# The expert stage: weights given back and loaded in pieces, in a new order of TensorE's work

## The reference

```
scores = sigmoid(x @ router.T)               # 32 experts, 4 chosen per token out of 3 of 8 groups
for each expert e: its first 10 tokens are taken (C = ceil(1.25 * 256 / 32) = 10), Xp[e] is 10 x 512
G = Xp @ W_gate[e]; U = Xp @ W_up[e]         # 512 x 256 each
Y = (silu(G) * U) @ W_down[e]                # 256 x 512
out[token] += weight * Y                     # scatter back
out += (silu(x @ sg.T) * (x @ su.T)) @ sd.T  # shared expert, hidden width 512
```

## Time and profile before

| | |
|---|---|
| median of 3 runs | 696.8 us (695.75 to 697.35) |
| profiled execution: its time, its span | 695.87 us, 694.0 us |
| mean granted clock of TensorE | 0.975 |
| busy: TensorE, VectorE, ScalarE, GpSimd | 631.8, 386.7, 360.5, 187.5 us |
| transfers over the whole span | 105.13 MB, 151 GB/s in the mean |
| expert stage, from the first row product to the end | 595.2 to 694.0 us |

### The profile page before, as it was taken

The page is one execution under the profiler, slowest core; times in us unless marked ns, Lnnn a source line. Parts: engine busy times, 40 slices in busy tenths (PEclk is TensorE's granted clock), DMA queues, the critical chain, the costliest instruction groups (busy, mean ns, idle before and its releaser), DMA issues.

```text
span 694.0 us, 14831 instructions
## 1 busy us (share of the span) xinstructions
PE 631.8 (91%) x5841; PEld 457.0 (66%) x5892; DVE 386.7 (56%) x536; ACT 360.5 (52%) x517; POOL 187.5 (27%) x151
## 2 busy tenths in 40 slices
PE   6999899999999999999999999999978988899855
PEld 5977666777777777777777777985546875553211
DVE  4869587767767677767677766341136854300001
ACT  3532766667666676667666766861126862110000
POOL 0250333443344334433442444440002220000000
PEclk9999999999999999999999999999989997999989
DMA  9934964324315305206215224009970051199993
GB/s 353 418 112 86 282 206 92 64 42 98 73 25 112 72 9 128 59 12 133 47 28 120 46 45 105 2 8 405 418 302 35 0 211 64 44 418 418 418 417 132
DMA packets 25511, 105.13 MB, mean 151 GB/s; under 512 B 3968, under 2 KB 7296, under 8 KB 19584
## 3 DMA queue, kind: packets, MB, share of 16 engines
q1 hardware_dynamic: 25472, 104.57, 46.1%
HBM read 77.29 MB, written 0.52 MB: 112 GB/s over the span
## 4 chain that ended last, share of the span: by engine, by line
PE 63%; DVE 14%; issue 10%; DMA 4%; SPq 4%; ACT 4%; POOL 1%; DVEq 0%; ACTq 0%
DVE arena L744 8%; PE psO L1044 6%; PE psM L994 6%; PE psO L1035 5%; PE psO L1036 5%; PE psS L1022 5%; PE psS L1023 5%; PE psO L1114 4%; SPq L366 4%; PE psO L979 3%; DMA arena<-w_exp 3%; PE psO L949 2%; PE psS L1255 2%; PE psS L957 2%; PE psO L980 2%
## 5 line engine op out<-in xcount | busy, mean ns | idle before, releaser
L707 DVE TENSOR_REDUCE arena<-psM 128x2 f32<-128x1024 f32 x121 | 148.3, 1225 | 80.9 <-PE psM L994 80.6
L425 POOL TENSOR_TENSOR arena<-arena 128x1024 bf16<-128x1024 f32 x64 | 138.4, 2163 | 147.5 <-ACT arena L531 143.5
L530 ACT ACTIVATE arena<-psS 128x1024 bf16<-128x1024 f32 x128 | 132.3, 1033 | 26.0 <-PE psS L1023 13.7
L1035 PE MATMUL psO<-arena 128*128 128x129 bf16 x1024 | 132.8, 220 | 1.5 <-ACT arena L530 1.2
L531 ACT ACTIVATE arena<-psS 128x1024 f32<-128x1024 f32 x128 | 132.6, 1036 | 0.0
L1036 PE MATMUL psO<-arena 128*128 128x128 bf16 x1024 | 132.3, 220 | 0.0
L1022 PE MATMUL psS<-arena 128*128 128x256 bf16 x512 | 120.5, 273 | 0.9 <-DVE arena L718 0.9
L1023 PE MATMUL psS<-arena 65*128 65x256 bf16 x512 | 120.8, 273 | 0.0
L1035 PEld LDWEIGHTS psO<-arena 128*128 128x128 bf16 x1024 | 99.1, 98 | 20.9 <-issue 12.7
L1036 PEld LDWEIGHTS psO<-arena 128*128 128x128 bf16 x1024 | 99.4, 97 | 6.7
L744 DVE TENSOR_TENSOR arena<-arena 128x1024 bf16<-128x1024 f32 x64 | 82.2, 1285 | 20.8 <-ACT arena L531 20.8
(11 more groups left out here) (188 smaller groups left out, 743.5 us busy)
## 6 DMA issues: line engine op xcount, KB each, us to landing
arena<-w_exp SPq DMA_DIRECT2D x32, 1024.0 KB, 17.1
arena<-arena SPq DMA_DIRECT2D x96, 256.0 KB, 3.8
arena<-w_exp SPq DMA_DIRECT2D x32, 512.0 KB, 17.9
arena<-w_pair SPq DMA_DIRECT2D x8, 1088.0 KB, 16.4
arena<-w_o SPq DMA_DIRECT2D x1, 4096.0 KB, 18.4
arena<-ctx SPq DMA_DIRECT2D x4, 512.0 KB, 12.9
arena<-rope SPq DMA_DIRECT2D x4, 512.0 KB, 13.6
arena<-w_shared_in SPq DMA_DIRECT2D x1, 2048.0 KB, 8.4
```

Of the source, the lines that this page charges most:

```text
L425: nc.gpsimd.tensor_tensor(p_lo[:, s % 2, :], p_f[:, s % 2, :], p_hi[:, s % 2, :], ALU.subtract).then_inc(s_plo[0], 1)
L530: nc.scalar.activation(p_hi[:, s % 2, :], psS[s % 2][:, :], ACT.Exp).then_inc(s_phi, 1)
L707: nc.vector.reduce_max(maxes[:, :, st, c], maxima_bank(q, m)[:, :].rearrange("p (j n) -> p j n", j=2), AX.X).then_inc(s_mfree, 1)
L1035: mm(psC[:, st, :], ph, vx[:, GROUP * g + i, 0:CW], start=g == 0 and i == 0 and st == 0, stop=False, skip_group_check=True)
```

## The change

1. **Row products and gate-up are interleaved.** TensorE starts a row product when the first half of the one-hot is there, and does gate-up of group 0 quarter by quarter, one row product behind. Group 1's gate-up follows at once; shared products 1 and 2 come behind down(0) and down(1), shared product 3 and weights_by_slot into group 2, shared_out(0 to 3) into groups 3 to 6.
2. **The first two groups give back quarters.** SyncE loads experts 13 to 20 (the places of groups 0 and 1) as 32 transfers of 256 KB, each quarter as soon as its gate-up quarter is done (`gu_part`); then the eight down parts, then expert 12, which now comes after both groups. Experts 21 to 28 are loaded as before.
3. **The last three experts** (29 to 31) come as 4 x 3 quarters of gate-up and 2 x 3 column halves of down (256 KB each, two runs of 1 KB in a row), each with a semaphore of its own, and gate-up of group 7 waits by quarters.
4. **The last trio is done in column halves**: down of groups 6 and 7 writes columns 0 to 255 into `psA[0]` and 256 to 511 into `psA[1]`; copy, combine, sum and store go by column halves. For this `psO[n]` now holds a column half of all tokens instead of a half of the tokens, also for the earlier combines and `shared_out` (four matmuls of 256 columns in place of two of 512). Shared banks are changed to match.
5. Pairs of semaphores are merged (`ld_out`, `ld_route`, `x_done`, `back_mm`, `back_copied`).

```diff
+PIECED = 2 * GE
+ENDING = RING + 4 * GE
+def gate_up_loaded(k):
+    if k < RING + PIECED:
+        return 16 if k < RING else 16 + 16 * DC
+    return 16 * (k // RING + 1) + (16 * (DC - 1) if k % RING < PIECED else 0)
...
-        sh_bank = [psF[0], psF[1], psO[0], psO[1]]
+        sh_bank = [psF[0], psO[0], psO[1], psO[0]]
...
-            for g in range((E - RING + GE - 1) // GE):
-                new = range(RING + GE * g, min(RING + GE * (g + 1), E))
+            def load_gate_up(k, c, done):
+                part = slice(2 * FI * c, 2 * FI * (c + 1))
+                sp.dma_start(ring[k % RING][:, part], a["w_exp"][expert(k)][:, part]).then_inc(done, 16)
+
+            def load_down(k, n, done):
+                part = [t[:, down].rearrange("p (c n) -> p c n", c=FC)[:, :, D // 2 * n:D // 2 * (n + 1)] for t in (ring[k % RING], a["w_exp"][expert(k)])]
+                sp.dma_start(part[0], part[1]).then_inc(done, 16)
+            for g in range(PIECED // GE):
+                for c in range(DC):
+                    if c < DC - 1:
+                        sp.wait_ge(gu_part, (DC - 1) * g + c + 1)
+                    else:
+                        sp.wait_ge(gu_mm, g + 1)
+                    for k in new(g):
+                        load_gate_up(k, c, ld_gu[k % RING])
+            for g in range(PIECED // GE):
+                sp.wait_ge(y_mm, g + 1)
+                for k in new(g):
+                    load_expert(k, down, ld_down)
+            sp.wait_ge(sh_mm, SH_FREES)
+            load_whole(RING_MID + 1)
+            for g in range(PIECED // GE, (ENDING - RING) // GE):
                 sp.wait_ge(gu_mm, g + 1)
...
-                if g == 0:
-                    sp.wait_ge(sh_mm, SH_FREES)
-                    load_whole(RING_MID + 1)
-            for s in range(TT):
-                sp.wait_ge(x3_done, s + 1)
...
+            sp.wait_ge(gu_mm, (ENDING - RING) // GE + 1)
+            for c in range(DC):
+                for k in range(ENDING, E):
+                    load_gate_up(k, c, ld_end_gu[c])
+            sp.wait_ge(y_mm, (ENDING - RING) // GE + 1)
+            for n in range(2):
+                for k in range(ENDING, E):
+                    load_down(k, n, ld_end_down[n])
+            for n in range(2):
+                half = slice(D // 2 * n, D // 2 * (n + 1))
+                sp.wait_ge(x3_done, n + 1)
+                sp.dma_start(out.rearrange("a (s p) d -> p (a s) d", p=P)[:, :, half], x[:, :, half]).then_inc(stored, 16)
...
+            def summed_last(n):
+                half = slice(D // 2 * n, D // 2 * (n + 1))
+                dve.wait_ge(y_mm, NG + n)
+                nc.vector.tensor_copy(y[:, (TRIOS - 1) % 2, half], psA[n][:, half]).then_inc(y_copied, 1)
...
+            dve.wait_ge(comb_mm, 1)
+            for n in range(2):
+                summed_last(n)
+            for n in range(2):
+                half = x[:, :, D // 2 * n:D // 2 * (n + 1)]
+                dve.wait_ge(comb_mm, TRIOS + n)
+                nc.vector.tensor_tensor(half, psO[n][:, :].rearrange("p (s d) -> p s d", s=TT), half, ALU.add).then_inc(x3_done, 1)
...
-            pe.wait_ge(oh_done, TT)
             pe.wait_ge(cleared, 2)
-            for c in range(DC):
+            def chosen_rows(c):
                 wait(pe, xp_copied, c - 1)
                 for st in range(TT):
+                    if c == 0:
+                        pe.wait_ge(oh_done, st + 1)
...
+            def gate_up(g, c):
+                if g == 0:
+                    pe.wait_ge(xp_copied, c + 1)
+                    if c == 0:
+                        pe.wait_ge(sh_done, 1)
+                if c == 0:
+                    wait(pe, hid_done, g - 1)
                 for j in range(GE):
                     k = GE * g + j
-                    pe.wait_ge(ld_gu[k % RING], 16 * (k // RING + 1))
-                for c in range(DC):
...
+                    if k < ENDING:
+                        pe.wait_ge(ld_gu[k % RING], gate_up_loaded(k))
+                    else:
+                        pe.wait_ge(ld_end_gu[c], 16 * (E - ENDING))
...
+                if c == DC - 1:
+                    last.then_inc(gu_mm, 1)
+                elif g < PIECED // GE:
+                    last.then_inc(gu_part, 1)
...
+                for n in range(2 if trio == TRIOS - 1 else 1):
+                    if g == NG - 1:
+                        pe.wait_ge(ld_end_down[n], 16 * (E - ENDING))
+                    bank, out = (psA[n], slice(D // 2 * n, D // 2 * (n + 1))) if trio == TRIOS - 1 else (psA[trio % 2], slice(0, D))
...
+            chosen_rows(0)
+            for c in range(1, DC):
+                chosen_rows(c)
+                gate_up(0, c - 1)
+            gate_up(0, DC - 1)
+            gate_up(1, 0)
+            gate_up(1, 1)
+            hidden_back(0)
+            gate_up(1, 2)
+            gate_up(1, 3)
+            down(0)
+            hidden_back(1)
+            shared_hidden(1)
+            down(1)
+            shared_hidden(2)
+            for g in range(2, NG):
+                for c in range(DC):
+                    gate_up(g, c)
+                if g == 2:
+                    shared_hidden(3)
+                    weights_by_slot()
+                elif g < 3 + DC:
+                    shared_out(g - 3)
                 hidden_back(g)
...
+            for n in range(2):
+                combine_last(n)
```

More of the change, by code:

```diff
@@ L352, in _ @@
             sp.dma_start(w_a, a["w_a"]).then_inc(ld_wa, 16)
[L353 to L356, removed]
+            sp.dma_start(w_router, a["w_router"]).then_inc(ld_route, 16)
+            sp.dma_start(bias_e, a["e_bias"].partition_broadcast(P)).then_inc(ld_route, 16)
+            sp.dma_start(wkv, a["w_kv"]).then_inc(ld_out, 16)
+            sp.dma_start(wo1, a["w_o1"]).then_inc(ld_out, 16)
             with sp.Fori(1, NPAIR) as q:
@@ L597, in _ @@
                     exps(i - 1)
-            act.wait_ge(o2T_mm, 1)
-            nc.scalar.copy(xnT.rearrange("p c s -> p (c s)"), psS[0][:, :]).then_inc(o2T_copied, 1)
+            act.wait_ge(back_mm, 1)
+            nc.scalar.copy(xnT.rearrange("p c s -> p (c s)"), psS[0][:, :]).then_inc(back_copied, 1)
             std(3)
@@ L665, in normalised, with residual @@
                                         ALU.subtract, ALU.mult).then_inc(ln_xn, 1)
-            def residual(s, bank, done):
-                nc.vector.tensor_tensor(x[:, s, :], bank[:, :], x[:, s, :], ALU.add).then_inc(done, 1)
-                dve.wait_ge(done, s + 1)
+            def residual(n, s, bank):
+                nc.vector.tensor_tensor(x[:, s, :], bank[:, :], x[:, s, :], ALU.add).then_inc(x_done, 1)
+                dve.wait_ge(x_done, TT * (n - 1) + s + 1)
             dve.wait_ge(ld_x, 16)
@@ L836, in _ @@
             dve.wait_ge(sig_exp, 1)
[L837 removed]
+            dve.wait_ge(ld_route, 32)
             sc, scb, sel = te(2), te(3), te(4)
@@ L1125, in _ @@
                 last.then_inc(qa_mm, 1)
-            pe.wait_ge(x1_done, TT)
+            pe.wait_ge(x_done, TT)
             for c in range(DC):
@@ L1187, in _ @@
                     last = nc.tensor.transpose(psS[0][:, T * c + P * st:T * c + P * st + P], xn[:, st, P * c:P * c + P], ident)
-            last.then_inc(o2T_mm, 1)
-            pe.wait_ge(o2T_copied, 1)
+            last.then_inc(back_mm, 1)
+            pe.wait_ge(back_copied, 1)
             pe.wait_ge(ld_wo2, 16)
@@ L1196, in _ @@
             xn_transposes(3)
-            pe.wait_ge(ld_router, 16)
+            pe.wait_ge(ld_route, 32)
             for st in range(TT):
@@ L1202, in _ @@
             last.then_inc(logit_mm, 1)
+            halves = [slice(D // 2 * n, D // 2 * (n + 1)) for n in range(2)]
             def shared_hidden(i):
@@ L1216, in shared_out @@
                 for st in range(TT):
-                    mm(psO[st][:, :], hs[:, i, P * st:P * st + P], sd[:, i, :], start=i == 0, stop=False)
+                    for n in range(2):
+                        mm(psO[n][:, D // 2 * st:D // 2 * (st + 1)], hs[:, i, P * st:P * st + P], sd[:, i, halves[n]],
+                           start=i == 0 and st == 0, stop=False, skip_group_check=True)
             shared_hidden(0)
@@ L1301, in _ @@
                     combine(0)
+                elif g == 6:
+                    combine(1)
                 down(g)
-                if g == 0:
-                    shared_hidden(2)
-                elif g == 1:
-                    weights_by_slot()
-            combine(TRIOS - 1)
+            for n in range(2):
+                combine_last(n)
 def constants():
```

123 lines of the change are left out of this document (59 added, 64 removed).

## The result

| | before | changed |
|---|---|---|
| median of 4 runs | 696.98 us | 688.87 us |
| ratio, 95% interval | | 0.9871 [0.9835, 0.9907] |
| profiled execution: time, span | 695.87, 694.0 us | 687.77, 685.8 us |

One of the changed kernel's four runs took 1035.5 us at a mean granted clock of 0.56 and is left out of the ratio but not of the median of 688.87 us; the other three took 685.43, 687.77 and 689.97 us, so their median is 687.77. Two later sets, each beside its own runs of the kernel before, gave 689.04 against 695.51 us (0.9895 [0.9869, 0.9920]) and 689.03 against 695.55 us (0.9895 [0.9870, 0.9919]). The gain is about 1%, 6.5 us by the medians of the two later sets, and in all three sets the interval lies clear of no change; 689.7 us was forecast.

The account below looks back on a forecast made before the run. The expert stage was taken as bound by its DMA stream: start 6.0 us earlier, pieces +3.4, work after landing 14.7 to 6.5, so 7.1 us less. Forecast median 689.7 us, own range 687.5 to 692, 8-in-10 range 686.5 to 693.0.

Parts of the forecast that it names:

- Start, 6.0 us sooner: Head of expert stage: first issue needs two row products and one gate-up quarter, so at 597.95 instead of 603.95.
- The stream stays fed: After the first issue: quarter releases keep the DMA engines supplied, the second release in time by 0.5 us.
- a sign of being wrong: Start of the stream: the forecast is wrong if DMA share falls below 0.95 in the first 20 us.
- Expert 12 late, harmless: Group 3: expert 12's gate-up lands near 635.5, TensorE stands still some 5 us, yet is not the bound.
- Pieces, +3.4 us: Expert stream: 2 KB rows add 2.8 us and 1 KB rows 0.6 us; last transfer lands at 680.4.
- the other sign of being wrong: Tail: the forecast is wrong if gate-up of group 7 ends after 678.
- After the landing, 14.7 to 6.5 us: Tail: after the last landing only a down half, two combine halves, sum and store remain, 6.5 us.
- (1): Expert stage: pieces cost nothing and TensorE sets the end; 8.3 us less, 688.5 us; chance 0.17.
- (2): Stream or tail: pieces cost up to 7 us, or the slow clock holds; 692.7 or 693.3 us; chance 0.15.
- (3): SyncE: its issues become the bound, slower than before, 703 us; chance 0.05.
- (4): Expert stream: a transfer's fixed part is serial, 2.0 us per 256 KB, 751 us; chance 0.01.
- (5): Expert stage: no difference, as slow engines, 1 KB store rows and half matmuls eat the gain; 695.5 to 698; chance 0.04.

Follow-up runs that it names:

- experiment 1: Changed kernel with experts 13 to 20 loaded as whole gate-ups, TensorE's new order kept: 96.3 us from the one-hot, ratio to before 0.9957.
- experiment 2: Changed kernel with the last three experts loaded whole, computation by column halves kept: 94.6 us from the one-hot, ratio to before 0.9914.
- experiment 4: Changed kernel with expert 12 queued after group 0's downs instead of after both groups': 93.85 us from the one-hot, ratio to before 0.9902.
- experiment 3: Kernel before with only experts 13 to 20's gate-ups loaded as 32 quarters, released no sooner: 102.9 us from the one-hot, ratio to before 1.0027.
- experiment 6: Changed kernel with fewer, larger pieces (54 transfers instead of 76), group 1 loaded whole: 91.9 us from the one-hot, ratio to before 0.9890.
- experiment 7: Kernel of experiment 6 with expert 12's gate-up queued after group 0's downs: 95.7 us from the one-hot, ratio to before 0.9908.

## Why the prediction was right

Its sum was 7.1 us of the stage; 6.5 were measured. The mechanism (start of the stream, price of the pieces, work after the last landing) stands. The parts that could be undone by themselves account for 3.0 us (experiment 1) and 1.35 us (experiment 2); the other 2.1 of the 6.5 us are read from rows, not isolated by a run.

- **Start, 6.0 us sooner.** 9.7 - 4.1 = 5.65. The missing 0.35 lies mainly in TensorE's start, 0.64 us after the one-hot's instead of 0.49, and in a gate-up quarter that took 0.99 to the next product instead of 0.91. The first row products were as long as said (1.08 by their copies); between gate-up quarters they took 1.27. Experiment 1 takes the early start away and pays 3.0, which is 5.4 of start less 2.4 of pieces.
- **The stream stays fed.** Share 0.94 and 0.99 in the first windows: no hole, but 313 to 351 GB/s, which I had not forecast. The 0.94 of the first 2 us of flow lies under the 0.95 that was named as a sign of being wrong, and so does the first microsecond alone (0.92); from 602 on it is 1.00 and more, so the sign was set too tight for a stream that is just starting.
- **Expert 12 late, harmless.** Group 3 was to start at 635.5, 41.3 after the one-hot; it started 43.0 after it, since the stream had run slower, idle 7.1 us instead of 5, and then took 5.56 us (5.68 forecast). The end did not see it (experiments 1 and 4).
- **Pieces, +3.4 us.** From first issue to last landing 79.0 us before, 82.8 after: +3.8. The row taken from the store, 87.6 ns for 2 KB, was the right one: 88.1 in the stream. By parts: 2.4 to 2.8 for the 32 quarters (experiments 1 and 3), 1.3 for the 18 transfers at the end (experiment 2). The 1 KB pieces cost 12 ns more each, where I took 6. Start and pieces together put the last landing 86.9 us after the one-hot, 0.7 later than forecast, and that is the 0.6 by which the sum missed. The end of group 7's gate-up, counted so, is at 84.0, just past the other sign of being wrong (678, or 83.8 after the one-hot).
- **The serial 2 us.** Experiment 3 has 24 more transfers and ends 3.1 us later. The Trainium skill's fit stands in "DMA: Bandwidth & Descriptors", section "Anatomy of one DMA — SWDGE (gpsimd) path", not in "Bandwidth" as the prediction says, and is for transfers issued by GpSimd, while these are issued by SyncE; the page calls the fixed part mostly completion latency. Taken as serial it would have put experiment 3 48 us later; by the 3.1 us, queued transfers share it.
- **After the landing, 14.7 to 6.5 us.** 6.3. The halves took 1.07 and 1.94.
- **Rivals.** TensorE as the bound (1) was not the case, by 1 us of wait before quarter 3, and is nearly so as soon as the stream gets shorter (experiment 6). The slow clock (2) occurs in the changed kernel in one of three profiles and costs 1.25 us in the tail, and 1.6 in the head, where I had not looked for it. (3), (4) and (5) did not occur: issues of 256 KB took SyncE 0.34 to 0.43 us where there was room, experiment 3 is against (4), and the stage's 6.5 us against (5).

That the median of 688.87 us lies only 0.8 from the forecast is in part luck. It is the mean of 687.77 and 689.97 us, and the first of these, the profiled execution, lies 1.9 under the forecast with a stage 0.6 us longer than forecast. In that execution what lies ahead of the stage was 1.6 us shorter, which no term of the sum foresaw. In the two later sets the difference to before is 6.5, as in the stage.

## What to carry to other kernels

Where a stage is a stream at the DMA engines' rate, as this one, three things set its time: when the first transfer can be issued, what each piece adds (here 8.5 ns a 2 KB row on each engine, 12 ns a 1 KB row), and the work after the last landing. Cut small only where it moves one of them: the first quarters and the last one; the other small pieces here cost 2 us of stream, and without them the stage was not longer (experiment 6). A stall in the middle cost nothing here, since its places came free before the queue was empty (experiments 1 and 4); removing it moved idleness towards the end, where it counts. And look at the second-longest path before making the longest one shorter: here they lay 0.1 us apart, and taking 2.1 us off the stream brought 1.3 in the profile.

## What the runs showed that I had not expected

- **Same program, same stage, two clocks.** 93.25 and 93.27 us with the granted clock at 1.00, 96.1 with 0.50 at the row products and in the last downs. TensorE had done the same work before in all three, and waited the same 1.72 us before the row products. Nor does the length of a wait alone tell: after 2.87 us of idleness group 7's gate-up ran at the full clock in experiment 2 (3.64 us), after 2.61 at the slow one in experiment 7 (5.15 us). The Trainium skill, "TensorE: Matmul & The Clock Gate", section "Part 1: The HAM clock gate (the "warmup" mystery)", says that the point of transition varies from run to run of the same kernel; these runs agree.
- **DMA engines end apart.** The last of the 16 engines end 2 us after most of them (three engines until 682.5 before; shares of 0.31 and 0.18 after), 4 us in experiment 7. Here every wait on a landing paid for the latest engine. The queue of instruction fetches moves 3 to 5 packets of 16 KB in this stage beside the stream; whether they set the lag was not tried.
- **Where the time of a run varies.** The start of the same row, with the same work before it, lies from 591.6 to 595.6 us. A gain of 1 us in this stage can't be seen in a median of six runs; it can in the stage's own rows, as long as the granted clock in them is the same.
